# Eight subtractions of a graph-attention kernel's head 3 change from Pool to VectorE

## The reference

```python
h = (x @ W).reshape(N, H, C)
e = leaky_relu(al_s[src] + al_d[dst], 0.2)
ex = exp(e - segment_max(e, dst)[dst])
alpha = ex / (segment_sum(ex, dst)[dst] + 1e-16)
out = segment_sum(h[src] * alpha[:, :, None], dst)
...
h = elu(gat_layer(x, src, dst, W1, ..., concat=True))      # 4 heads of 512 columns
out = gat_layer(h, src, dst, W2, ..., concat=False)        # 1 head of 768 columns
return layernorm(x + out)
```

## Time and profile before

| | before |
|---|---|
| median of 3 runs | 955.25 us (954.58 to 955.36) |
| profiled execution, time | 957.13 us |
| profiled execution, span | 955.3 us |
| mean granted TensorE clock | 0.977 |
| PE / VectorE / ScalarE / Pool busy | 887.2 / 606.9 / 424.1 / 223.3 us |

### The profile page before, as it was taken

The page is one execution under the profiler, slowest core; times in us unless marked ns, Lnnn a source line. Parts: engine busy times, 40 slices in busy tenths (PEclk is TensorE's granted clock), DMA queues, the critical chain, the costliest instruction groups (busy, mean ns, idle before and its releaser), DMA issues.

```text
span 955.3 us, 15152 instructions
## 1 busy us (share of the span) xinstructions
PE 887.2 (93%) x5719; PEld 800.6 (84%) x5719; DVE 606.9 (64%) x1155; ACT 424.1 (44%) x686; POOL 223.3 (23%) x148
## 2 busy tenths in 40 slices
PE   4997885999999999999999998989999999699996
PEld 2455553889888998889988897989999999699996
DVE  9547743658893698828887388663222344397887
ACT  5346433257643675437663385852111111387300
POOL 1000003035321243122431266500000000154452
PEclk9999897999999999999999999999999999889999
DMA  8508994553467334582164333446232441400223
GB/s 299 134 1 119 151 169 134 137 151 132 158 193 189 121 115 139 170 202 95 38 193 117 103 132 121 135 142 150 54 84 47 78 75 30 98 3 2 59 88 97
DMA packets 64451, 111.19 MB, mean 116 GB/s; under 512 B 31772, under 2 KB 33464, under 8 KB 63004
## 3 DMA queue, kind: packets, MB, share of 16 engines
q1 hardware_dynamic: 64379, 110.22, 45.1%
HBM read 85.25 MB, written 24.94 MB: 115 GB/s over the span
## 4 chain that ended last, share of the span: by engine, by line
PE 65%; DVE 12%; issue 8%; POOL 6%; ACT 3%; SPq 3%; DMA 2%; DVEq 1%; POOLq 0%; ACTq 0%
PE ps L1683 19%; PE ps L1685 18%; PE ps L1684 18%; POOL pbuf L586 5%; PE ps L1714 3%; PE ps L1655 2%; DVE pbuf L599 2%; PE ps L1804 2%; SPq L656 2%; PE ps L1645 1%; DVE h2f L1594 1%; DMA w1raw<-in_L_gnn_W 1%; DVE h2f L1568 1%; DVE ring L1338 1%; DVE vbuf L1413 1%
## 5 line engine op out<-in xcount | busy, mean ns | idle before, releaser
L586 POOL TENSOR_TENSOR pbuf<-pbuf,grow 125x625 f32<-125x625 f32 x100 | 170.4, 1704 | 549.0 <-ACT pbuf L571 248.8
L1683 PE MATMUL ps<-hx,PThi 125*125 125x260 f32 (+5 forms) x800 | 228.2, 285 | 6.7 <-DVE vbuf L1407 3.8
L1685 PE MATMUL ps<-hx,PTlo 125*125 125x260 f32 (+5 forms) x800 | 225.9, 282 | 0.0
L1684 PE MATMUL ps<-hlo,PThi 125*125 125x260 f32 (+4 forms) x800 | 225.6, 282 | 0.0
L1683 PEld LDWEIGHTS ps<-hx,PThi 125*125 125x125 f32 x800 | 149.4, 187 | 11.3 <-DVE PTlo L613 3.5
L1684 PEld LDWEIGHTS ps<-hlo,PThi 125*125 125x125 f32 x800 | 149.8, 187 | 1.5
L1685 PEld LDWEIGHTS ps<-hx,PTlo 125*125 125x125 f32 x800 | 149.7, 187 | 0.0
L599 DVE SCALAR_TENSOR_TENSOR pbuf<-pbuf,counts 125x625 f32<-125x625 f32 x100 | 98.6, 986 | 25.3 <-ACT pbuf L593 25.1
L1683 PE MATMUL ps<-W2p,hT 128*125 128x384 f32 x320 | 109.7, 343 | 3.2 <-DVE hT L1419 1.7
L608 ACT ACTIVATE PThi<-pbuf 125x625 fp32r<-125x625 f32 x80 | 57.8, 723 | 114.4 <-DVE pbuf L599 57.5
L1685 PE MATMUL ps<-W2p,hT 128*125 128x384 f32 x320 | 108.1, 338 | 0.0
(11 more groups left out here) (187 smaller groups left out, 1611.4 us busy)
## 6 DMA issues: line engine op xcount, KB each, us to landing
xr<-xT_scratch SPq DMA_DIRECT2D x30, 750.0 KB, 4.7
nbm<-mask_scratch SPq DMA_DIRECT2D x40, 273.4 KB
hidden_scratch<-vbuf SPq DMA_DIRECT2D x40, 224.0 KB
hblk<-hidden_scratch SPq DMA_DIRECT2D x10, 896.0 KB
xT_scratch<-xa SPq DMA_DIRECT2D x20, 375.0 KB, 11.5
w1f<-in_L_gnn_W SPq DMA_DIRECT2D x12, 512.0 KB, 9.3
w1raw<-in_L_gnn_W SPq DMA_DIRECT2D x4, 1536.0 KB, 7.9
w2raw<-in_L_gnn_W SPq DMA_DIRECT2D x14, 384.0 KB, 5.1
```

Source lines behind the costliest of these rows:

```text
L586: pool.tensor_tensor(pslot(c), pslot(c), src[:, g * GN:(g + 1) * GN], ALU.add).then_inc(e_done, 1)
L1683: pe.matmul(dst, ahi, bhi, start=start, stop=False, skip_group_check=shared)
L1684: pe.matmul(dst[:, 0:n], ahi, blo, start=False, stop=False, skip_group_check=shared)
L1685: return pe.matmul(dst, alo, bhi, start=False, stop=stop, skip_group_check=shared)
```

## The change

VectorE gets a `split_w2` with the same subtraction and the same counter, and Pool loses it. VectorE runs it one chunk later than Pool did: at b = 4 to 9 in group 0 and at b = 7 and 9 in group 1 of head 3, at the end of the iteration, after the ELU step where there is one. ScalarE, SP and TensorE are as before.

```diff
--- before.py
+++ after.py
@@ -897,11 +897,6 @@
-            def split_w2(c):
-                pool.wait_ge(w2_hi, c + 1)
-                pool.tensor_tensor(W2p[:, c, 1, :], w2_raw(c), W2p[:, c, 0, :].bitcast(F32), ALU.subtract
-                                   ).then_inc(w2_lo_p, 1)
-
@@ -911,11 +906,6 @@
                 if c + 2 < CHUNKS:
                     pool_add(pool, c + 2)
-                if g == 0 and 3 <= b < 3 + KD:
-                    if h + 1 == H:
-                        split_w2(b - 3)
-                if h == H - 1 and g == 1 and b in (6, 8):
-                    split_w2(b // 2 + 3)
@@ -1318,6 +1308,10 @@
+            def split_w2(c):
+                dve.wait_ge(w2_hi, c + 1)
+                dve.tensor_tensor(W2p[:, c, 1, :], w2_raw(c), W2p[:, c, 0, :].bitcast(F32), ALU.subtract).then_inc(w2_lo_p, 1)
+
@@ -1443,6 +1437,10 @@
                 if g == 0 and 4 <= b < 4 + KD and h + 1 < H:
                     split_w1(h + 1, b - 4)
+                if h == H - 1 and g == 0 and 4 <= b < 4 + KD:
+                    split_w2(b - 4)
+                if h == H - 1 and g == 1 and b in (7, 9):
+                    split_w2(b // 2 + 3)
```

## The result

| | before | after |
|---|---|---|
| median | 954.61 us (952.65 to 955.36, 6 runs) | 948.38 us (947.27 to 951.03, 6 runs) |
| ratio | | 0.9943 (95%: 0.9928 to 0.9958) |
| profiled execution: time, span | 957.13, 955.3 us | 947.27, 945.4 us |
| mean granted TensorE clock | 0.977 | 0.984 |
| first matmul of chunk 60 | 550.67 | 545.79 |

The kernel is 0.57% faster, 5.4 us by the ratio, 6.2 by the medians. Of the 9.9 us between the two profiled spans, 5.9 lie between chunk 60 and chunk 71. 4.9 lie ahead of chunk 60, where the two kernels are the same program, and 0.9 go the other way behind chunk 71 (from there to the last matmul with W2 both take 221.7 us, so the 0.9 lie behind that). So the change is read from chunk 60 to 71, and the rest is told of at the end.

A forecast was written before the change was run, and what follows sets the result against it. VectorE, taking turns with Pool on SBUF operands, was taken to bound head 3, group 0. Chunk 71 comes 5.84 us earlier, group 1 costs 0, sum −5.8: 955.25 − 5.8 = 949.4 us, range 947.8 to 952.3.

The forecast's parts named there:

- VectorE and Pool in turns: Head 3, group 0: the engines exclude each other on SBUF operands; a chunk costs about their sum, 5.2 us.
- Pool's queue: Rival from the experiments, no chance given: Pool's add waits behind whatever Pool runs; chunk 60 to 71 about 46.7 us.
- The schedule taken over from head 2: Head 3, group 0: head 2's 24.39 us plus 1.62; eviction at 585.59, chunk 71 5.84 us earlier.
- The six times 0.27: Head 3, group 0: six W2 splits of 768 columns each take 0.27 us more than head 2's 512-column W1 splits.
- The clock: Around chunk 70: no stretch at 1.2 GHz expected, with TensorE busy up to 586; granted clock 1.00 from 590 to 600.
- the 1.3 at stake: From the eviction to chunk 71: up to 1.3 us of the gain come back if the 1.2 GHz stretch stays.
- The chunks before chunk 70 are fed: Head 3, group 0: with steps of 4.0 to 4.3 us the three-chunk lead shrinks to some 1.5 us, not used up.
- Group 1 at nothing: Head 3, group 1: two moved splits cost 0, up to 1 us if the covers are gone.
- Chunk 77's lead: Group 1: called the thinnest lead, 1.87 us; TensorE coming 1.3 closer leaves 0.6, but Pool's delaying part is gone.
- The turns didn't eat the gain: Rival, head 3, group 0: Pool's add waits among four VectorE instructions; gain 2, time 953.1; chance 0.06 for part eaten.
- VectorE never went ahead of it for several instructions: Slower rival, head 3, group 0: VectorE instructions precede Pool's add, 5.6 us per chunk, time 959.8; chance 0.05.
- Nothing was given back: Rival, after the last eviction: stores, loads or W2 tiles aren't there, 5 us lost, 954.4; chance 0.09 with all eaten.

The follow-up runs named there:

- the instruction that only writes: Kernel after, plus a Pool instruction at the six old group 0 places that reads nothing and writes unused memory: 947.41 us, ratio 0.9929 to before.
- group 1 alone: Kernel after, but Pool keeps the six splits of group 0 and only group 1's two go to VectorE: 953.92 us, ratio 1.0003 to before.
- group 0 alone: Kernel after, but Pool keeps the two splits of group 1 and only group 0's six go to VectorE: 949.16 us, ratio 0.9961 to before.
- the second time: The kernel after, unchanged, run again beside a later experiment: 949.84 us, ratio 0.9947 to before.
- the doubled subtractions: Kernel after, with each of group 0's six subtractions made twice on VectorE: 958.55 us, ratio 1.0048 to before.

## Why the prediction was right

- **What bounds head 3, group 0.** Right: VectorE and Pool in turns. The rival that I tested against it, Pool's queue, is out by the instruction that only writes.
- **The schedule taken over from head 2.** From chunk 60 the eviction was to start 34.92 us later (585.59 less 550.67); it started 34.79 later (580.58 less 545.79). Chunk 71 was to start 40.90 later and did so 40.83 later; part of that closeness is luck, as the eviction came 0.13 early and the step behind it took 0.06 longer. The gain in the stretch is 5.91, predicted 5.84. The six times 0.27 for the wider tile, 1.62, were about the right size: from the low part of b = 4 to the eviction it is 25.87 (554.71 to 580.58), 1.48 more than head 2's 24.39.
- **Chunk 70** starts 36.20 after chunk 60. I had VectorE 0.79 late against 35.69; it was 0.51 late.
- **The clock.** I expected no stretch at 1.2 GHz, and there is none. From the eviction's start to chunk 71 it takes 6.04 (580.58 to 586.62), against 7.29 before and 5.98 in head 2. Of the 1.3 at stake 1.25 were won.
- **The chunks before chunk 70 are fed.** Right: no wait for low parts; the steps are 4.28, 4.26, 4.01, 4.25, 3.65 and 2.33, near the 4.0 to 4.4 forecast as long as the ELU is in them. The lead shrinks to 2.0 us, where I had some 1.5. VectorE's busy time in lines 613, 599 and 1413 (now 1407) falls as said, from 79.3, 98.6 and 43.8 to 76.8, 91.2 and 41.0.
- **Group 1 at nothing.** Right: 29.42 us from chunk 71 to 79 in both, and the kernel with group 1 alone shows no change. Chunk 77's lead, for which I had left 0.6 and whatever Pool's missing split gives, is 1.6: its low part ends at 606.46, TensorE starts at 608.05. With Pool's split left in (group 0 alone) it is 0.6, as reckoned. But chunk 77 was not the thinnest, as I had read it. Chunk 71's low part, made behind the eviction, had 1.78 before (595.63 to 597.41), less than the 1.87 of chunk 77, and has 0.5 now (586.10 to 586.62). I had overlooked it. It held; had TensorE needed 0.6 us less behind the eviction, it would have waited there.

```profile
585.30 0.80 DVE L613 TENSOR_TENSOR PTlo<-pbuf,PThi 125x625 fp32r<-125x625 f32 x1
...
605.65 0.81 DVE L613 TENSOR_TENSOR PTlo<-pbuf,PThi 125x625 fp32r<-125x625 f32 x1 [1.83 <-ACT PThi L608]
...
608.05 0.29 PE L1681 MATMUL ps<-hx,PThi 125*125 125x260 f32 x1
```

- **The rivals.** The turns didn't eat the gain: Pool's add got its turn once per step, and VectorE never went ahead of it for several instructions. Nothing was given back up to the last matmul with W2: from chunk 71 to there it takes 221.7 us in both. The 0.9 behind it is not explained.
- **The whole time.** Predicted 949.4, measured 948.38. The 5.8 fits both the ratio (5.4, from 4.0 to 6.9) and the medians (6.2), but this agreement is coarser than that of the stretch, for the reason that the last section tells.

## What to carry to other kernels

When a VectorE instruction with two operands in SBUF takes two or three times its usual time, look for a Pool instruction that ends just before it: add the two engines' work on SBUF operands up as if it were one engine's, and compare that sum with what TensorE needs per step. Moving work from Pool to VectorE pays in such a stretch when VectorE does it in less time (here 0.87 for 1.85), though VectorE is the busier of the two. The same step in another loop of the same kernel is the best price list: head 2's schedule plus six times the difference in width gave the stretch to 0.1 us.

## What I had not expected

Ahead of head 3 all nine profiled executions run the same program, and they differ by nearly what this change is worth. Chunk 60 starts at 550.67 in the kernel before, at 545.79 and the second time at 549.24 in the kernel after, and between 545.96 and 549.69 in the other six. Behind chunk 71 they differ less, 357.9 to 359.1, and none of that lies ahead of the last matmul with W2.

What goes with the start of chunk 60 is the granted clock ahead of it, in the part that builds the matrix of counts. TensorE's window from 30 to 160 us, before and after (busy time, clock, DMA share, GB/s):

```profile
30.00:160.00 130.00, 103.95 (x582) 0.91 0.68 112
```

```profile
30.00:160.00 130.00, 107.56 (x617) 0.95 0.66 117
```

The nine fall in line: 0.95 where chunk 60 starts at 545.79, 545.96 and 546.00, 0.93 at 547.81, 0.92 at 547.54, 548.71 and 549.24, and 0.91 at 549.69 and 550.67. The kernel after has both 0.95 and, the second time, 0.92, with chunk 60 3.45 us later. So most of this spread comes with the execution and not with the build, and the kernel before had a late one profiled. 0.04 of 130 us is 5.2 us of full clock, about the 4.9 by which the two profiles differ ahead of chunk 60; that is an estimate, and what sets the level in an execution no run here tells.

Nor is it told whether a small part goes with a build: the kernel with group 0 alone gained 3.7 us in the whole and 5.9 in the stretch; the one with the doubled subtractions lost 4.6 and 1.7. It is left open. So a change of this size is better read from the stretch that it touches: in the two profiles of the kernel after, that stretch is 40.83 both times, while the two executions differ by 3.6 us in the whole (947.27 and 950.86).
